# Moving a batch's last layernorm and store from the next batch's last heads to right behind its residual sum

## What is computed

```python
def _layernorm(x, axis=-1, eps=1e-05):
    m = jnp.mean(x, axis=axis, keepdims=True)
    v = jnp.var(x, axis=axis, keepdims=True)
    return (x - m) / jnp.sqrt(v + eps)

x = L0_attn_x
x = _layernorm(x + _L0_attn_ref(x, ...))      # gated convolution, then an MLP
x = _layernorm(x + _L0_ffn_ref(x, ...))       # 32 experts and a shared one
x = _layernorm(x + _L1_attn_ref(x, ...))      # 16 heads, causal softmax attention
x = _layernorm(x + _L1_ffn_ref(x, ...))       # silu(x wg) * (x wu), 2:4 sparsified, times wd
```

## Time and profile before

| | us |
|---|---|
| median of 3 runs | 1975.47 |
| lowest and highest of them | 1975.36, 1990.34 |
| the profiled execution, its own time | 1981.23 |
| its span (first to last instruction) | 1979.4 |
| mean granted TensorE clock in it (share of 2.4 GHz) | 0.903 |
| PE busy | 1680.2 |
| DVE busy | 1155.4 |
| ACT busy | 795.0 |
| POOL busy | 235.7 |

### The profile page before, as it was taken

One profiled execution on the slowest core, in us unless ns is written; L12 is line 12 of the kernel. 1 busy time (PEld: TensorE's weight loads), 2 busy tenths in 40 slices (PEclk: granted clock), 3 DMA queues, 4 the chain that ended last, 5 costly groups with the idle time before them and its releaser, 6 DMA issues.

```text
span 1979.4 us, 26413 instructions
## 1 busy us (share of the span) xinstructions
PE 1680.2 (85%) x10042; PEld 1025.4 (52%) x10043; DVE 1155.4 (58%) x2367; ACT 795.0 (40%) x1296; POOL 235.7 (12%) x237
## 2 busy tenths in 40 slices
PE   4999999877999965699889899789899879889897
PEld 3788888764568762233444433444433434433345
DVE  5566566536321235677466677656677556678364
ACT  5444444412212103277542267542167542167420
POOL 4333333311400001000100000100000100000000
PEclk8999999978999877599989889999988999989898
DMA  2000000005125302000000000000000000000000
GB/s 98 11 22 22 21 21 22 30 13 166 40 66 153 89 0 88 0 1 1 1 0 1 0 1 1 22 0 0 1 1 1 22 0 1 0 1 1 22 0 22
DMA packets 27147, 47.96 MB, mean 24 GB/s; under 512 B 7312, under 2 KB 16016, under 8 KB 26256
## 3 DMA queue, kind: packets, MB, share of 16 engines
q1 hardware_dynamic: 26464, 44.74, 7.0%
q0 software_dynamic: 576, 1.77, 0.3%
HBM read 37.59 MB, written 9.06 MB: 24 GB/s over the span
## 4 chain that ended last, share of the span: by engine, by line
issue 60%; POOL 2%; DVE 0%; POOLq 0%; DVEq 0%
POOL rs_sb L1324 1%; POOL ve_sb L1321 0%; POOL qks_sb L1339 0%; POOL v_sb L1338 0%; POOL qks_sb L1329 0%; DVE bn_sb L1504 0%; DVE x_sb_sb L1519 0%; POOLq L1159 0%; POOLq L65 0%; POOL qks_sb L1340 0%; DVE mv_sb L1510 0%; DVEq L1159 0%; POOL v_sb L1337 0%; DVEq L65 0%; DVEq L1508 0%
## 5 line engine op out<-in xcount | busy, mean ns | idle before, releaser
L1561 DVE TENSOR_REDUCE mx_sb<-s_ps 128x1 f32<-128x512 f32 (+1 forms) x512 | 322.2, 655 | 132.2 <-PE s_ps L1815 89.0
L1392 ACT ACTIVATE room_sb<-s_ps 128x1024 f32<-128x1024 f32 (+1 forms) x320 | 282.2, 948 | 20.7 <-PE s_ps L1839 18.0
L1812 PE MATMUL s_ps<-room_sb 48*128 48x512 f16 (+3 forms) x640 | 204.0, 348 | 18.3 <-DVE mx_sb L1556 9.8
L1839 PE MATMUL s_ps<-room_sb 51*128 51x128 f16 (+4 forms) x1152 | 151.4, 292 | 35.3 <-ACT room_sb L1392 27.1
L1859 PE MATMUL cm_ps<-room_sb,v_sb 128*32 128x512 f32 (+3 forms) x1536 | 175.1, 538 | 0.8 <-ACT room_sb L1398 0.8
L1812 PEld LDWEIGHTS s_ps<-room_sb 48*128 48x128 f16 x640 | 59.5, 98 | 223.4 <-DVE mx_sb L1561 131.8
L1321 POOL TENSOR_TENSOR ve_sb<-mv_sb,eps_sb 128x4 f32<-128x4 f32 x24 | 5.0, 210 | 1191.1 <-DVE mv_sb L1510 1191.1
L1971 PE MATMUL s_ps<-xbT_sb,w_fg_sb 128*128 128x512 f32 x256 | 132.7, 630 | 13.8 <-DVE room_sb L1607 13.0
L1984 PE MATMUL cm_ps<-w_fd_sb,room_sb 128*128 128x256 f32 x512 | 131.8, 406 | 14.2 <-DVE room_sb L1635 14.2
L1971 PE MATMUL s_ps<-xbT_sb,w_fu_sb 128*128 128x512 f32 x256 | 132.1, 628 | 0.0
L392 DVE SCALAR_TENSOR_TENSOR x_sb_sb<-xp_sb,conv_w_sb,x_sb_sb 128x512 f32<-128x512 f32 x96 | 108.5, 1139 | 22.8 <-ACT x_sb_sb L319 20.5
(11 more groups left out here) (239 smaller groups left out, 3295.9 us busy)
## 6 DMA issues: line engine op xcount, KB each, us to landing
we_gu_sb<-we_gu SPq DMA_DIRECT2D x32, 352.0 KB
we_dn_sb<-we_dn SPq DMA_DIRECT2D x32, 176.0 KB
x_in_sb<-x SPq DMA_DIRECT2D x9, 512.0 KB, 3.6
rows<-x_sb_sb SPq DMA_DIRECT2D x8, 512.0 KB, 3.0
x_sb_sb<-rows SPq DMA_DIRECT2D x2, 2048.0 KB, 11.4
out<-x_sb_sb SPq DMA_DIRECT2D x8, 512.0 KB, 2.6
xp_sb<-w_in SPq DMA_DIRECT2D x1, 1024.0 KB, 5.6
x_sb_sb<-w_up SPq DMA_DIRECT2D x1, 1024.0 KB, 6.7
```

Of the source, the lines that this page charges most:

```text
L1392: act.activation(weights[(g * NU + u) % SLOTS_P][:, 2 * pair:2 * pair + 2, 0:width(u) * P], W[s % 2][:, :, 0:width(u) * P], ACT.Exp, scale ...
L1561: dve.tensor_reduce(mx[:, pair, k % 2, slot:slot + 1], X[:, k % 2, 0:count * P], AX.X, ALU.max, negate=True).then_inc(mx_ok, 1)
L1812: last = pe.matmul(X[:, k % 2, at * P:(at + plain) * P], query[head:head + NORM, i * P:(i + 1) * P], key[head:head + NORM, j * P:(j + plai ...
L1839: last = pe.matmul(W[s % 2][:, head, (at + low - i) * P:(at + high - i) * P], key[first:first + rows, j * P:(j + 1) * P], query[first:firs ...
```

## The change

The layernorm "f" of both halves of batch b, and with it the two stores, move from the last group of `heads(b + 1)` to the end of batch b, right behind `residual(b, 1)`. This concerns b = 0, 1 and 2. In the freed steps of the last group the two "x" layernorms of the batch after stand at the steps 4 and 11 in place of 10 and 14. `ORDER` follows. For the last batch the order of instructions is as it was.

```diff
         ORDER = [("x", 0, 0), ("x", 0, 1)]
         for b in range(NB):
-            if b > 0:
-                ORDER += [("f", b - 1, 0), ("f", b - 1, 1)]
             if b + 1 < NB:
                 ORDER += [("x", b + 1, 0), ("x", b + 1, 1)]
-            ORDER += [("a", b, 0), ("a", b, 1)]
-        ORDER += [("f", NB - 1, 0), ("f", NB - 1, 1)]
+            ORDER += [("a", b, 0), ("a", b, 1), ("f", b, 0), ("f", b, 1)]
         LN = {key: k for k, key in enumerate(ORDER)}
...
                         if g == NHG - 1:
-                            if b > 0 and s in (2, 6):
-                                finish(b - 1, s // 4)
-                            if b + 1 < NB and s in (10, 14):
-                                layernorm("x", b + 1, s // 4 - 2)
+                            if b + 1 < NB and s in (4, 11):
+                                layernorm("x", b + 1, s // 7)
...
                     hidden(b, 15)
                     sparsify(b, 3)
                     maxima(c, 0, 28, 2 * NX)
-                    residual(b, 1)
-            finish(NB - 1, 0)
-            residual(NB - 1, 1)
-            finish(NB - 1, 1)
+                else:
+                    finish(b, 0)
+                residual(b, 1)
+                if ahead:
+                    finish(b, 0)
+                finish(b, 1)
```

## The result

The changed kernel is slower. Its median is 2006.47 us in 6 runs (1997.58 to 2008.3), against 1982.29 us in 6 runs of the kernel before (1975.36 to 1990.34). The ratio is 1.011, with a 95% interval of 1.0073 to 1.0147. A second set on another chip gave 2001.81 us in 6 runs against 1978.16 in 23, ratio 1.0104 (1.0074 to 1.0135). The ratios make 21.8 and 20.6 us, the medians differ by 24.2 and 23.7; the forecast was 25.7 us, or 1.013, which lies inside both intervals. As an absolute time the forecast was 2001.2 us, from a median before of 1975.47 in 3 runs; in the 6 runs above that median is 1982.29, and a change is to be judged against it. That 2006.47 lies next to rival (A)'s 2007.2 comes from this and says nothing for (A). The profiled execution took 2006.97 us, with a span of 2005.2, which is 25.8 us more than the span before.

A forecast was written before the change was run, and what follows sets the result against it. The prediction took the boundary to be bound by DVE, PE and ACT in sequence, not by PE's busy share. +26.4 + 0.9 - 1.6 = +25.7 us on a median of 1975.47 gave 2001.2 us, range 1994 to 2009.

The forecast's parts named there:

- rival (A): After the longer stall the clock stays low some 4 us again; three boundaries cost 6 us more, 2007.2 us; chance 0.18.
- What bounds the boundary: From residual to first exponential DVE, PE and ACT work one after the other; whoever is late is late for everyone.
- (B): Half of the stall is caught up in group 0 of the heads, 13 of 26 us; about 1988 us; chance 0.08.
- The sum: Whole kernel: +26.4 + 0.9 - 1.6 = +25.7 us, giving 2001.2 us, 1.3% slower.
- (C): The stall at the boundaries is hidden and only the last group's gain is left; 1973.9 us; chance 0.04.
- Part 1: Two layernorms on DVE at each of three boundaries delay the first maximum by 8.8 us each, 26.4 us in all.
- POOL's and SP's parts: At the boundary, POOL's four instructions per pair lie inside DVE's waits and SP's two stores delay nobody; both cost nothing.
- Part 2: First maximum to ACT's copy runs at the lower clock at all three boundaries after PE's idleness; 0.9 us more.
- The prediction's two rows: Granted clock 0.50 in 1130 to 1132 and 1.00 in 1430 to 1432, read as the same distance from the residual.
- I let this move along unchanged: The clock's return behind the boundary, some 4 us after the first weighted sums began, was taken to shift without cost.
- Part 3: In the last group DVE divides the sums sooner with two layernorms fewer; gain 1.37 + 0.27 = 1.64 us.

The follow-up runs named there:

- half dose: From the kernel before: only half 0's final layernorm moves to the boundary, half 1's stays in the last group; 1.0052 of the kernel before, 10.3 us over.
- shortened layernorms: Changed kernel with two sets of small tiles and both statistics ahead of both normalisations, POOL's part beside DVE's; 1.0054 of the kernel before, 10.7 us over.
- layernorm in the gap: From the kernel before: half 0's layernorm between DVE's last sparsification and the maxima from 28 on, half 1's in the last group; 0.9993 of the kernel before.

## Why the prediction was right, and where it was off

- **What bounds the boundary**: right. DVE, PE and ACT work one after the other there. The half dose and the shortened layernorms moved the first maximum by what was taken from the work ahead of it, and with the layernorms behind six maxima the wait moved to PE's ninth product. The rival that half of the stall is caught up because PE has work ready (B) has no support in the intervals: 5.86, 8.05 and 10.60 us for one, one and a half and two layernorms' worth of DVE's time, each passed on to ACT's copy in full. What the heads gave back behind the copy is under "The sum"; PE having work ready is not how. The rival that it is hidden (C) is refuted by PE's wait of 9.29 us.
- **Part 1, the stall**: 8.8 us forecast, 8.78 measured at all three boundaries. POOL's and SP's parts at nothing: right.
- **Part 2, first maximum to ACT's copy at the lower clock**: 3.97 us at all three, where it had been 3.98, 3.46 and 3.61; 0.9 forecast, 0.9 measured. But 9 us of idleness are not what brings the lower level. In the changed kernel's first trace the granted clock fell 1.7 to 2.2 us behind the residual, when PE had just begun to wait; in its second trace it fell 1.9, 4.5 and 2.0 us behind it, and in the kernel before 1.8, 4.6 and 4.3. The delay puts the whole stretch, from 10.6 us on, behind the fall wherever that is. Without a stall the stretch is as slow when the fall is early: 3.97 to 3.98 us at all three boundaries of the kernel without final layernorms and of the one with the layernorm in the gap. So the 0.9 holds against the falls in the trace of before, and against other executions it can be nothing. (The prediction's two rows stand 2.6 and 1.5 us behind their residuals, not at the same distance; the falls at 1.8 and 4.6 us bear its reading out.) "I let this move along unchanged", of the clock behind it, was wrong. The low stretch ended later: some 15 us behind the residual before, 25.6 to 26.0 us behind it now, which is 2 us more than the stall's 8.8. The first weighted sums began at 1153.12, and the clock was still 0.50 from 1144 to 1156 and 0.76 on average from 1156 to 1162, while before it came back some 4 us after them (the rows stand below this list). That much of rival (A) happened. Its price did not come, for the heads had less low clock later on: from 30 us behind the residual up to the context, summed over the three batches, 41 and 48 us in the two traces of the kernel before, 34 and 14 in the two of the changed one. From the copy to the context they took 124.8, 125.4 and 121.8 us in one execution and 121.7, 121.3 and 121.7 in the other, against 125.3, 127.0 and 122.8 before and 123.6 to 123.7 with no final layernorm at all. Why the clock falls less often later is open.
- **Part 3, the last group**: the intervals of 1.37 and 0.27 us are gone, as forecast; in the time they can't be seen.
- **The sum**: 25.7 forecast; 25.8 between the two first traces, of which 5.4 lay ahead of anything that the change moved, so that this agreement is luck. In the changed kernel's second trace batch 0's residual came at 1125.85, 1.6 us earlier than before. The runs say 21 to 22 us by the ratios and 24 by the medians. From batch 0's last residual to the end the two traces are 20.4 and 13.3 us over the kernel before, and the second of these is what rival (B) had as its number, though not by its mechanism. The term that was mis-sized is the clock's, as a term of the whole batch and not of the few us at the boundary: it was put at +0.9, and by the runs the heads and what follows gave back 2 to 5 us. With run-to-run differences this large the forecast's 25.7 isn't excluded either, so this remains likely and not shown.

The changed kernel's two stretches behind the first boundary, columns as above, granted clock third from the end:

```profile
1144.00:1156.00 12.00, 9.06 (x64) 3.89 (x63) 6.01 (x11) 6.08 (x6) 0.00 (x0) 0.50 0.11 44
1156.00:1162.00 6.00, 6.00 (x55) 2.35 (x52) 4.48 (x8) 3.21 (x5) 0.00 (x0) 0.76 0.01 3
```

## What to carry to other kernels

Where engines with queues of their own hand each other the first work of a stage, each one's lateness is everybody's: price an insertion there at its full occupied time, waits for a helper engine included, less the idleness that follows it on its own engine before somebody needs the next result. This gives the delay at that place; the kernel's time here rose by some 80 to 90% of the 26.4 us. Nothing in an engine's busy share shows it. Look for the same work's place at a wait of the same engine a few us earlier or later: the layernorm that made everybody 4 us late right behind the residual cost nothing that can be told 16 us ahead of it or behind six maxima. The last of these, with one layernorm moved and the other left, is 0.2 to 0.3% faster than the kernel before in two sets, on different chips. It has the lowest ratio of all those run, but both intervals end within 0.03% of no difference, and that of the kernel with the layernorm in the gap overlaps them.

## What the runs showed of the hardware that was not expected

- One kernel's executions differ by more than its small edits: 23 runs of the kernel before on one chip gave 1973.28 to 1989.24 us. Much of the difference goes with PE's granted clock: in the sets of 21 and 23 runs of the kernel before, the correlation of time and mean clock is -0.69 to -0.92. The Trainium skill, "TensorE: Matmul & The Clock Gate", section on the clock gate, has the interval over which activity is judged run free of the kernel, so that the moment of a change varies; the traces agree in that the moment varies: in the kernel before the clock fell 1.8, 4.6 and 4.3 us behind three equal residuals, and nearly equal stretches took 127 and 132 us at 0.95 and 0.88.
- A stretch in which PE was busy for 10.00 of 10 us by its modelled ends, with f16 matmuls of 48 by 128 on 48 by 512, stayed at 0.51. The same section takes sustained activity as what releases the clock; this run does not show it, and the measurement decides here.
- Why one layernorm behind the six maxima makes the kernel faster is open. In its first trace PE's granted clock from residual to context was 0.93, 0.95 and 0.95 at the three boundaries, low for 17, 14 and 14 us, in the one without final layernorms 0.89, low for 27 us each. The second trace of it did not show that advantage (123.7 to 123.8 us from copy to context, as without final layernorms), though its runs were again faster.
